# P times V with V as the loaded weights of four 32-column tiles, turned P streaming, and row sums from columns of ones

## The chip, the cores and the metric

One core of a Trainium2 chip runs the kernel; the other seven are idle. The metric is the time of one execution on the device in microseconds, the median of the runs. TensorE multiplies (one operand is loaded into the array as weights, the other streams through it), VectorE and ScalarE work on tiles in SBUF and PSUM, GpSimd on SBUF alone; the DMA queue is SyncE's.

## The reference

A cross attention and a gated feed-forward layer over 16 batches of 128 rows of width 1024, both with a residual. The attention has 32 heads of width 32 in 8 groups; the 4 heads of a group share K and V.

```python
x = x + xattn(layernorm(x), ctx, ctx, w_q, w_k, w_v, w_out, mask)
x = x + ffn(layernorm(x), w12, b12, w3, b3)

# xattn, per batch b, group g and head h of the group
scores = einsum('bghnd,bgsd->bghns', query, key) / 32 ** 0.5
scores = where(mask, scores, finfo.min)
attention = softmax(scores, axis=-1)
out = einsum('bghns,bgsd->bghnd', attention, value)
return out.transpose(0, 3, 1, 2, 4).reshape(b, n, 1024) @ w_out.T
```

The change is in `out`: softmax's division and the product with `value`.

## The kernel before

Every f32 operand is split into a high and a low f16 half, and a product is three f16 products: high by high, high by low, low by high. The kernel is written per engine, each with its own list of instructions and with semaphores between them; the order of the work is written out by hand, and is the same on all engines.

The attention runs over 8 blocks (t = 1 to 8) of U = 2 batches (256 rows), each in 8 steps s, one for each group. Group number g = 8 (t - 1) + s runs from 0 to 63. In a step TensorE does, in this order: `scores(g)` (8 matmuls, one for each batch and head, into the bank pair B_SCORE), a first product of 24 matmuls (q, o or v: a projection or the output projection of an earlier block), `turn_attn(g - 3)` at L1362, a second product, and `weigh(g - 2)` at L1412. In the last step of a block (s = 7) the two products are the two batches of the V projection, four `turn_x` calls turn the next rows, and in blocks 1 to 6 `turn_top` (L1329) and `spread_top` (L1337) turn a column of maxima into a row and spread one value over all partitions. In block 8 and three steps after it the first feed-forward products take the place of the projections. Then follow the last output projection and the feed-forward layer.

`weigh(g)` before: for each of the 2 batches and 4 heads it loads P turned (128 x 128, high and low half) as weights and streams V (32 columns, and in `v_high` a 33rd column of ones that makes the row sum), so that the result lies in B_AV with rows on partitions, 33 columns a head. It waits for the turned P (a DMA transpose), and for `s_avread`, which says that the division of the group before has read B_AV.

`divide(g)` at L1833 on VectorE: a reciprocal of the 8 row sums, then a multiplication of 256 columns into `attn` (f32, SBUF). `turn_attn(g)` transposes `attn` on TensorE into a PSUM bank, `attn_hi(g)` on ScalarE copies it as f16 into `attn_t`, `attn_lo(g)` on VectorE writes the rest that f16 lost. `out_proj(b, q)` reads `attn_t` of the 8 groups of a block as weights.

In a step VectorE does, in order: `divide(g - 3)`, `mask_scores(g)` (8 custom instructions, L1820), `gather_top` where there is one, for g up to 11 its share of `prob_lo(g - 1)` (L1830; from then on GpSimd does it all), the low half of the first product (`q_lo`, `k_lo`, `v_lo`, all L1790, or `residual`), `attn_lo(g - 3)`, extra work of some steps (`max_of`, `row_stats`, `o_low`), the low half of the second product, and `take_top`. ScalarE does the exponentials of the first batch, the high half of the first product, `attn_hi(g - 3)`, the exponentials of the second batch, the high half of the second product, and `prob_hi(g)`.

TensorE's results of all products and turns go round five PSUM banks (`banks()`, L218): a table worked out ahead gives each key in `dense_order()` (L174) the bank that has been free or held longest, and `begin` (L1319) waits until VectorE has read that bank's last content. The key ("a", g) is the turn of group g. Keys that are gone from the list change the banks of all later ones.

## Time and profile before

| | |
|---|---|
| time, median of 3 runs | 1041.52 us (1041.49 to 1042.86) |
| span of the profiled execution | 1040.4 us |
| TensorE busy | 1017.7 us (98%) |
| VectorE busy | 661.6 us (64%) |
| ScalarE busy | 447.3 us (43%) |
| GpSimd busy | 498.6 us (48%) |
| granted TensorE clock | 0.998 of full |

The time of the profiled execution is not given apart from its span, which runs from the first to the last instruction; the median of the runs is 1.1 us above it. Busy time is the time in which at least one instruction of the engine is under way. Matmuls overlap: a row with "x8" and a duration is the whole run of 8, and from one start to the next is what a matmul costs in a stream.

### The profile page before, as it was taken

How to read it: one execution, taken by the hardware profiler on the slowest of the kernel's cores; microseconds unless marked ns; L12 is line 12 of the kernel's file. 1: busy time of each engine (PE TensorE's matmuls, PEld its weight loads, DVE VectorE, ACT ScalarE, POOL GpSimd, SP SyncE). 2: the span in 40 equal slices, each digit the busy share in tenths (PEclk: the TensorE clock that was granted, in tenths of full speed). 3: DMA queues.
4: the chain of work that ended last, by engine and by line, in shares of the span. 5: the costliest groups of instructions: out<-in, count | busy, mean ns of one | idle time of the engine just before them, and what ended most of it. 6: DMA issues, size and time to landing. Idle time of an engine off the chain costs nothing.

```text
span 1040.4 us, 21876 instructions
## 1 busy us (share of the span) xinstructions
PE 1017.7 (98%) x8400; PEld 695.6 (67%) x8400; DVE 661.6 (64%) x2080; ACT 447.3 (43%) x983; POOL 498.6 (48%) x476
## 2 busy tenths in 40 slices
PE   7897999999999999999999999999999999999998
PEld 6786868869687696886655544444444888468853
DVE  6789977767787777888646234636864447625431
ACT  6768556557465574664766210123431112202100
POOL 2869923727337273379958596158742301212000
PEclk9999999999999999999999999999999999999999
DMA  9669686998989999789946715494758631974201
GB/s 367 227 160 197 168 216 168 222 247 222 248 211 229 230 245 244 179 236 232 268 94 123 253 71 203 94 345 160 272 200 185 235 112 40 236 230 122 83 31 51
DMA packets 230776, 199.12 MB, mean 191 GB/s; under 512 B 177040, under 2 KB 187280, under 8 KB 225808
## 3 DMA queue, kind: packets, MB, share of 16 engines
q1 hardware_dynamic: 230672, 197.72, 69.0%
q8 instruction: 67, 1.10, 0.4%
q14 instruction: 37, 0.30, 0.1%
HBM read 119.04 MB, written 35.65 MB: 149 GB/s over the span
## 4 chain that ended last, share of the span: by engine, by line
PE 87%; DVE 6%; DMA 1%; ACT 1%; issue 0%; SPq 0%; DVEq 0%
PE bank_dense L1349 52%; PE bank_spare L1349 13%; PE bank_score L1494 6%; PE bank_spare L1494 6%; PE bank_av L1494 3%; PE bank_score L1406 2%; DVE arena_attn L1820 2%; DVE arena_attn L1830 1%; PE bank_av L1424 1%; PE bank_av L1428 1%; PE bank_av L1426 1%; PE bank_dense L1366 1%; DMA k_scratch<-arena_in 1%; PE bank_spare L1358 0%; PE bank_dense L1358 0%
## 5 line engine op out<-in xcount | busy, mean ns | idle before, releaser
L1153 ACT ACTIVATE arena_attn<-arena_attn,arena_in 128x128 f32<-128x128 f32 x512 | 162.7, 391 | 94.6 <-DVE arena_in L1820 93.6
L1349 PE MATMUL bank_dense<-arena_rows,arena_in 128*128 128x256 f16 (+1 forms) x1272 | 175.2, 295 | 1.9 <-POOL arena_in L874 1.0
L936 POOL TENSOR_TENSOR arena_attn<-arena_attn 128x512 f16<-128x512 f32 x89 | 102.6, 1170 | 148.8 <-ACT arena_attn L1160 148.8
L1349 PE MATMUL bank_dense<-arena_attn,arena_rows 128*128 128x512 f16 x768 | 166.4, 379 | 0.0
L1349 PEld LDWEIGHTS bank_dense<-arena_rows,arena_in 128*128 128x128 f16 x1272 | 123.0, 98 | 43.1 <-DVE arena_in L1668 1.6
L1820 DVE CUSTOM_DVE_ANT_0 arena_attn<-bank_score,arena_in 128x128 f32<-128x128 f32 x512 | 143.5, 346 | 0.4 <-PE bank_score L1406 0.4
L1349 PEld LDWEIGHTS bank_dense<-arena_attn,arena_rows 128*128 128x128 f16 x768 | 75.2, 98 | 90.2
L1349 PE MATMUL bank_dense<-arena_out,arena_attn 128*128 128x512 f16 x576 | 127.8, 379 | 0.0
L1349 PEld LDWEIGHTS bank_dense<-arena_out,arena_attn 128*128 128x128 f16 x576 | 55.5, 98 | 63.3
L1349 PE MATMUL bank_spare<-arena_rows,arena_in 128*128 128x256 f16 (+1 forms) x648 | 87.6, 292 | 0.0
L1349 PE MATMUL bank_dense<-arena_out,arena_in 128*128 128x512 f16 x384 | 83.0, 379 | 0.0
L874 POOL TENSOR_TENSOR arena_in<-arena_in 128x512 f16<-128x512 f32 x62 | 74.2, 1196 | 5.0
L1349 PEld LDWEIGHTS bank_spare<-arena_rows,arena_in 128*128 128x128 f16 x648 | 63.0, 98 | 19.0
L1907 DVE SCALAR_TENSOR_TENSOR arena_out<-bank_dense,small,arena_out 128x256 f32<-128x256 f32 x64 | 28.0, 478 | 75.0 <-PE bank_dense L1349 75.0
L884 POOL TENSOR_TENSOR small<-small 128x1 f32<-128x1 f32 x32 | 19.9, 622 | 107.2 <-DVE small L1709 107.2
L1349 PEld LDWEIGHTS bank_dense<-arena_out,arena_in 128*128 128x128 f16 x384 | 37.6, 98 | 45.3
L1160 ACT ACTIVATE arena_attn<-arena_attn 128x1024 f16<-128x1024 f32 x64 | 67.2, 1050 | 1.0 <-DMA arena_attn<-arena_attn 0.7
L1349 PE MATMUL bank_dense<-arena_in 128*128 128x256 f16 x456 | 52.8, 273 | 1.4 <-DVE arena_in L1675 1.4
L1424 PE MATMUL bank_av<-v_high,arena_attn 128*128 128x33 f16 x512 | 45.5, 178 | 6.7 <-DMA arena_attn<-arena_attn 6.7
L1003 POOL TENSOR_TENSOR arena_out<-arena_out,arena_rows 128x1024 f32<-128x1024 f32 x12 | 29.2, 2462 | 47.1 <-DMA arena_out<-x_scratch 47.1
L1859 DVE SCALAR_TENSOR_TENSOR arena_rows<-bank_dense,small,arena_rows 128x256 f32<-128x256 f32 x48 | 21.0, 479 | 46.9 <-PE bank_dense L1349 43.9
L1349 PEld LDWEIGHTS bank_dense<-arena_in 128*128 128x128 f16 x456 | 43.8, 98 | 7.8 <-DVE arena_in L1675 1.7
(219 smaller groups left out, 1890.8 us busy)
## 6 DMA issues: line engine op xcount, KB each, us to landing
arena_rows<-x SPq DMA_DIRECT2D x32, 512.0 KB, 6.1
arena_in<-w_scratch SPq DMA_DIRECT2D x64, 256.0 KB, 3.1
arena_attn<-q_scratch SPq DMA_DIRECT2D x48, 256.0 KB, 4.5
arena_rows<-w_t SPq DMA_DIRECT2D x12, 1024.0 KB, 6.2
arena_rows<-ctx_t SPq DMA_DIRECT2D x8, 1024.0 KB, 6.1
q_scratch<-arena_attn SPq DMA_DIRECT2D x16, 512.0 KB, 5.1
x_scratch<-arena_rows SPq DMA_DIRECT2D x16, 512.0 KB, 3.8
arena_out<-x_scratch SPq DMA_DIRECT2D x16, 512.0 KB, 5.9
```

The source lines that it names most:

```text
L874: pool.tensor_tensor(lo, buf, hi, ALU.subtract).then_inc(ready, 1)
L936: ins = pool.tensor_tensor(p_split[:, g % 2, u, 1], e[:, g % 2, u], p_split[:, g % 2, u, 0], ALU.subtract)
L1003: ins = pool.tensor_tensor(y_res[:, u], y_res[:, u], b3_all, ALU.add)
L1153: ins = act.activation(head, head, ACT.Exp, bias=neg_max[:, g % 2, h:h + 1], scale=-1.0)
L1160: act.activation(p_split[:, g % 2, :, 0], e[:, g % 2], ACT.Copy).then_inc(s_phi, 1)
L1349: ins = pe.matmul(dst, lhs(a, c), rhs(b, c), start=(c == chunks[0] and n == 0), stop=(c == chunks[-1] and n == 2))
L1406: ins = pe.matmul(B_SCORE[:, HALF * u + SEQ * j:HALF * u + SEQ * j + SEQ], q_stack[0:3 * DH, m // 4, j, m % 4, SEQ * u:SEQ * u + SEQ], k_s ...
L1424: pe.matmul(B_AV[:, at:at + VW], prob_t[:, g % 2, u, 0, j], v_high[:, a % 2, u, m], start=True, stop=False)
L1494: ins = pe.matmul(seven(v, j), weights[:, a, P * c:P * c + P], rows[:, b, c], start=(c == 0 and n == 0), stop=(c == 3 and n == 2))
L1820: ins = dve.tensor_tensor_reduce(out=e[:, g % 2, h // HPG, SEQ * (h % HPG):SEQ * (h % HPG) + SEQ], in0=B_SCORE[:, SEQ * h:SEQ * h + SEQ], ...
L1859: ins = dve.scalar_tensor_tensor(out=cols, in0=bank("o", b, q)[:, 256 * n:256 * n + 256], scalar=c_out[:, 2 * h + n:2 * h + n + 1], in1=co ...
L1907: ins = dve.scalar_tensor_tensor(out=cols, in0=bank("y", f, q)[:, 256 * k:256 * k + 256], scalar=c_ffn[:, 2 * h + k:2 * h + k + 1], in1=co ...
```

## The change

- `weigh(g)` loads V as weights instead of P: for each batch the three products of the output (V high with P high, V high with P low, V low with P high) and two of the row sums (a block of 32 columns of ones with P high and with P low). Each is done for the 4 heads in 4 tiles of 32 columns of the array: head j writes partitions 32 j to 32 j + 31 of B_AV, 128 columns wide. The weights are 128 x 32, the streaming side is P turned, 128 x 128. That is 40 matmuls a group instead of 24. The outputs lie in columns 0 to 255 of B_AV, the sums, the same on all 32 partitions of a head, in columns 256 to 511.
- The result has heads and their columns on partitions, as `out_proj` reads it, so `turn_attn` is gone, with its entries in the orders.
- `divide(g)` takes the reciprocal of 128 x 256 sums (into `inv_rows`) and multiplies 128 x 256.
- `attn_hi(g)` and `attn_lo(g)` read `attn` in SBUF, with two semaphores of their own (`s_ahi`, `s_alo`); `out_proj` and `late_hi` wait for `s_alo`.
- `v_high` has 32 columns a group; the ones are a block of their own, set once by GpSimd.

```diff
--- before.py
+++ after.py
...
@@ -187,8 +186,6 @@
                 n.append(("h", 0, H_AT[s], 0))
-            if g >= 3:
-                n.append(("a", g - 3))
             if tile2 is not None:
@@ -198,7 +195,7 @@
     for s in (8, 9, 10):
-        n += [("h", 0, H_AT[s], 0), ("a", NG - 11 + s), ("h", 0, H_AT[s], 1)]
+        n += [("h", 0, H_AT[s], 0), ("h", 0, H_AT[s], 1)]
     n += [("o", NB - 1, q) for q in range(4)]
@@ -259,7 +256,7 @@
 SPREADS = [*FIRST_TOPS, *(key[1] for key in dense_order() if key[0] == "turn")]
-HIGHS = [key for key in dense_order() if key[0] in ("x", "a", "q", "k", "v")]
+HIGHS = [key for key in dense_order() if key[0] in ("x", "q", "k", "v")]
 
@@ -407,13 +404,15 @@
         kept, with_6, with_5, with_7 = [terms[:, 0], terms[:, 1]], terms[:, 2], terms[:, 3], terms[:, 4]
+        inv_rows = part(arena_attn, 59, 1, F32)
+        ones_wide = part(arena_attn, 60, 1)[:, 0:DH]
         k_stack = part(arena_attn, 63, 4).rearrange("p (b g n) -> p b g n", b=2, g=4)
         temp_late = part(arena_attn, 63, 2, F32)
-        v_high = sb("v_high", [P, 2, U, GROUPS, VW], F16)
+        v_high = sb("v_high", [P, 2, U, GROUPS, DH], F16)
         v_low = sb("v_low", [P, 2, U, GROUPS, DH], F16)
...
         stage.append(v_low.rearrange("p r u g w -> p (r u g w)").rearrange("p (s n) -> p s n", s=2))
-        stage.append(v_high.rearrange("p r u g w -> p (r u g w)")[:, 0:2 * HALF].rearrange("p (s n) -> p s n", s=2))
+        stage.append(v_high.rearrange("p r u g w -> p (r u g w)").rearrange("p (s n) -> p s n", s=2))
 
...
@@ -920,7 +920,7 @@
                 root(r)
-            pool.memset(v_high[:, :, :, :, DH:DH + 1], 1.0).then_inc(s_vinit, 1)
+            pool.memset(ones_wide, 1.0).then_inc(s_wide, 1)
             pool.wait_ge(*taken("q23"))
@@ -1119,10 +1119,10 @@
             def attn_hi(g):
-                act.wait_ge(s_dense, done("a", g))
+                act.wait_ge(s_avread, g + 1)
                 if g >= RING:
                     act.wait_ge(s_dense, done("o", (g - RING) // GROUPS, 3))
-                act.activation(attn_t[:, g % RING, 0], bank("a", g)[:, 0:AB], ACT.Copy).then_inc(s_dhi, 1)
+                act.activation(attn_t[:, g % RING, 0], attn, ACT.Copy).then_inc(s_ahi, 1)
 
@@ -1180,7 +1180,7 @@
                 act.wait_ge(s_w12, 28)
-                act.wait_ge(s_dense, done("a", NG - 1))
+                act.wait_ge(s_alo, NG)
                 act.activation(w12[:, 7, :, 0].rearrange("p i c o -> p i (c o)"),
...
@@ -1359,13 +1358,6 @@
 
-            def turn_attn(g):
-                pe.wait_ge(s_avread, g + 1)
-                dst = begin("a", g)
-                for u in range(U):
-                    ins = pe.transpose(dst[:, P * u:P * u + P], attn[:, P * u:P * u + P], ident[:, :])
-                ins.then_inc(s_dense, 1)
-
             def q_proj(t, m):
@@ -1418,21 +1410,22 @@
                     pe.wait_ge(*taken("ctx1"))
+                    pe.wait_ge(s_wide, 1)
                 for u in range(U):
-                    for j in range(HPG):
-                        at = VW * (HPG * u + j)
-                        pe.matmul(B_AV[:, at:at + VW], prob_t[:, g % 2, u, 0, j], v_high[:, a % 2, u, m],
-                                  start=True, stop=False)
-                        pe.matmul(B_AV[:, at:at + DH], prob_t[:, g % 2, u, 0, j], v_low[:, a % 2, u, m],
-                                  start=False, stop=False)
-                        ins = pe.matmul(B_AV[:, at:at + VW], prob_t[:, g % 2, u, 1, j], v_high[:, a % 2, u, m],
-                                        start=False, stop=True)
+                    terms_of_out = ((v_high[:, a % 2, u, m], 0), (v_high[:, a % 2, u, m], 1), (v_low[:, a % 2, u, m], 0))
+                    terms_of_sum = ((ones_wide, 0), (ones_wide, 1))
+                    for at, wanted in ((0, terms_of_out), (AB, terms_of_sum)):
+                        for n, (weights, piece) in enumerate(wanted):
+                            for j in range(HPG):
+                                ins = pe.matmul(B_AV[DH * j:DH * j + DH, at + SEQ * u:at + SEQ * u + SEQ], weights,
+                                                prob_t[:, g % 2, u, piece, j], start=n == 0, stop=n == len(wanted) - 1,
+                                                tile_position=(0, DH * j))
                 ins.then_inc(s_av, 1)
...
                 if q == 0:
-                    pe.wait_ge(s_dread, done("a", GROUPS * b + 7))
+                    pe.wait_ge(s_alo, GROUPS * b + 8)
                 if b == 0 and q == 0:
@@ -1561,8 +1554,6 @@
                         hidden(0, H_AT[s], 0)
-                    if g >= 3:
-                        turn_attn(g - 3)
                     if tile2 is not None:
@@ -1576,7 +1567,6 @@
                 hidden(0, H_AT[s], 0)
-                turn_attn(NG - 11 + s)
                 if s < 10:
@@ -1831,18 +1821,14 @@
             def divide(g):
-                av = B_AV[:, 0:VW * U * HPG].rearrange("p (h w) -> p h w", w=VW)
                 dve.wait_ge(s_av, g + 1)
-                dve.reciprocal(inv_sum[:, :].rearrange("p (h o) -> p h o", o=1), av[:, :, DH:DH + 1]).then_inc(s_inv, 1)
+                dve.reciprocal(inv_rows, B_AV[:, AB:2 * AB]).then_inc(s_inv, 1)
                 dve.wait_ge(s_inv, g + 1)
-                dve.tensor_tensor(attn.rearrange("p (h w) -> p h w", w=DH), av[:, :, 0:DH],
-                                  inv_sum[:, :].rearrange("p (h o) -> p h o", o=1).broadcast_to([P, U * HPG, DH]),
-                                  ALU.mult).then_inc(s_avread, 1)
+                dve.tensor_tensor(attn, B_AV[:, 0:AB], inv_rows, ALU.mult).then_inc(s_avread, 1)
 
             def attn_lo(g):
-                dve.wait_ge(s_dhi, hi_count("a", g))
-                dve.tensor_tensor(attn_t[:, g % RING, 1], bank("a", g)[:, 0:AB], attn_t[:, g % RING, 0], ALU.subtract)\
-                   .then_inc(s_dread, 1)
+                dve.wait_ge(s_ahi, g + 1)
+                dve.tensor_tensor(attn_t[:, g % RING, 1], attn, attn_t[:, g % RING, 0], ALU.subtract).then_inc(s_alo, 1)
```

## Rows read from the trace of the kernel before

**Rows 1.** The page's first part: busy us (share of the span) x instructions.
```profile
PE 1017.7 (98%) x8400; PEld 695.6 (67%) x8400; DVE 661.6 (64%) x2080; ACT 447.3 (43%) x983; POOL 498.6 (48%) x476
```

**Rows 2.** Busy time by stretch; columns as the first line names them.
```profile
core 0: us, PE busy (x) PEld busy (x) DVE busy (x) ACT busy (x) POOL busy (x), PEclk, DMA share, GB/s
73.00:129.00 56.00, 47.58 (x601) 41.92 (x599) 54.16 (x201) 39.52 (x99) 52.23 (x51) 1.00 0.86 188
129.00:610.00 481.00, 480.46 (x4633) 340.95 (x4634) 336.52 (x1376) 274.34 (x673) 268.94 (x282) 1.00 0.84 212
610.00:1040.00 430.00, 426.92 (x2643) 258.31 (x2640) 217.10 (x367) 84.90 (x132) 137.45 (x102) 1.00 0.52 158
```

**Rows 3.** The chain that ended last, 126 to 133 us: start, us, what.
```profile
128.24 0.13 DVE arena_in L1836
128.38 0.44 DVE arena_in L1838
...
128.87 0.44 PE bank_spare L1366 x2
129.30 2.62 PE bank_dense L1349 x24
```

**Rows 4.** Timeline of TensorE, weigh(8): start us, us, engine, line, operation, count.
```profile
131.76 0.18 PE L1424 MATMUL bank_av<-v_high,arena_attn 128*128 128x33 f16 x1
131.79 0.18 PE L1426 MATMUL bank_av<-v_low,arena_attn 128*128 128x32 f16 x1
131.81 0.18 PE L1428 MATMUL bank_av<-v_high,arena_attn 128*128 128x33 f16 x1
...
132.37 0.61 PE L1406 MATMUL bank_score<-arena_attn 96*128 96x128 f16 x8
```

**Rows 5.** Timeline of TensorE, 302.0 to 302.6 us, around one turn_attn.
```profile
302.24 0.38 PE L1366 MATMUL bank_dense<-arena_in 128*128 128x128 f32 x2
302.46 0.38 PE L1358 MATMUL bank_spare<-arena_in,arena_rows 128*128 128x128 f32 x2
```

**Rows 6.** Timeline of TensorE, 298.0 to 298.9 us, scores, turn_top, product.
```profile
298.19 0.61 PE L1406 MATMUL bank_score<-arena_attn 96*128 96x128 f16 x8
298.64 0.28 PE L1335 MATMUL bank_spare<-arena_in 128*1 128x128 f32 x1
298.75 0.38 PE L1349 MATMUL bank_spare<-arena_in 128*128 128x256 f16 x2
```

**Rows 7.** Weight loads by form: count | busy us, mean ns | idle before.
```profile
L1366 PEld LDWEIGHTS bank_dense<-arena_in 128*128 128x128 f32 x84 | 11.1, 141 | 5.0 <-DVE arena_in L1838 0.2
L1335 PEld LDWEIGHTS bank_spare<-arena_in 128*1 128x1 f32 x7 | 0.6, 84 | 0.0
```

**Rows 8.** Timeline of TensorE, 240.9 to 241.7 us, around one spread_top.
```profile
240.74 0.60 PE L1349 MATMUL bank_dense<-arena_in 128*128 128x256 f16 x4
241.27 0.38 PE L1342 MATMUL bank_dense<-small,arena_in 1*128 1x2 f32 x2
241.58 0.19 PE L1424 MATMUL bank_av<-v_high,arena_attn 128*128 128x33 f16 x1
```

**Rows 9.** VectorE by form: count | busy us, mean ns | idle before.
```profile
L1838 DVE TENSOR_TENSOR arena_in<-bank_av,arena_in 128x256 f32<-128x256 f32 x64 | 27.1, 424 | 2.2
L1836 DVE RECIPROCAL arena_in<-bank_av 128x8 f32<-128x8 f32 x64 | 12.7, 199 | 1.1
L1887 DVE RECIPROCAL small<-small 128x8 f32<-128x8 f32 x1 | 0.2, 205 | 0.0
L1895 DVE RECIPROCAL small<-small 128x1 f32<-128x1 f32 x1 | 0.2, 165 | 0.0
L1886 DVE TENSOR_SCALAR small<-small 128x8 f32<-128x8 f32 x1 | 0.2, 158 | 0.0
L1890 DVE TENSOR_SCALAR small<-small 128x1 f32<-128x1 f32 x1 | 0.2, 153 | 0.0
```

**Rows 10.** Timelines of VectorE and ScalarE in a short step, last product's halves.
```profile
320.07 0.42 DVE L1790 SCALAR_TENSOR_TENSOR arena_attn<-bank_dense,arena_attn 128x256 f16<-128x256 f32 x1 [2.06 <-ACT arena_attn L1131]
...
319.65 0.39 ACT L1131 ACTIVATE arena_attn<-bank_dense 128x256 f16<-128x256 f32 x1 [1.00 <-PE bank_dense L1349]
```

**Rows 11.** Timelines of VectorE and TensorE, last step of block 4.
```profile
302.26 0.41 DVE L1790 SCALAR_TENSOR_TENSOR v_low<-bank_spare,v_high 128x256 f16<-128x256 f32 x1
...
303.39 2.79 PE L1349 MATMUL bank_dense<-arena_in 128*128 128x256 f16 x24
```

More of the change, by code:

```diff
@@ L49 @@
 EPS = 1e-5
-VW = DH + 1
 EXPONENT = 0x7F800000
@@ L534, in xattn_ffn @@
         s_pool = sem("pool_chain")
-        s_ident, s_ones, s_vinit, s_mask_add = sem("ident_done"), sem("ones_done"), sem("v_init_done"), sem("mask_done")
+        s_ident, s_ones, s_wide, s_mask_add = sem("ident_done"), sem("ones_done"), sem("wide_ones_done"), sem("mask_done")
         s_rload = [sem("even_rows_loaded"), sem("odd_rows_loaded")]
@@ L559, in xattn_ffn @@
         s_av, s_inv, s_avread = sem("av_done"), sem("inv_sum_done"), sem("attn_ready")
+        s_ahi, s_alo = sem("attn_hi_done"), sem("attn_lo_done")
         s_scales, s_cout = sem("block_scales_done"), sem("c_out_done")
@@ L1228, in _ @@
             o_sum(3)
-            act.wait_ge(s_vinit, 1)
             v_hi(0, 0)
```

## The prediction, made before the changed kernel was run

> **What bounds the kernel now.** I read the page's first part, then busy time by stretch, then the chain that ended last. TensorE is busy 1017.7 of 1040.4 us [rows 1], but a share over the whole span says little about one stage. By stretch [rows 2] there are three regimes. From 73 to 129 us VectorE is busy 54.16 of 56.00 us and TensorE 47.58: the first attention steps are VectorE's. From 129 to 610 us TensorE is busy 480.46 of 481.00 and VectorE 336.52: a microsecond of TensorE work is a microsecond of time there, and VectorE has air. From 610 us on nothing that the diff touches runs. The chain says the same and names the hand-over [rows 3]: VectorE's pieces follow each other until the division of group 7 at 128.38, for which turn_attn(7) waits at 128.87; from there it is TensorE to the end. So there are two accounts: VectorE work in the first 8 divisions (groups 0 to 7), TensorE work in the 56 calls of weigh after the hand-over (groups 8 to 63) and the 57 turns (groups 7 to 63).
>
> **What goes from TensorE.** weigh(8) starts at 131.76 and the scores after it at 132.37 [rows 4]: 24 matmuls with their 24 weight loads in 0.61 to 0.62 us, a start every 25.5 to 25.8 ns, although one matmul lasts 177 ns: they are pipelined. A turn of one group starts at 302.24 and the next work at 302.46 [rows 5]: 0.22 us. So 56 x 0.62 = 34.7 us and 57 x 0.22 = 12.5 us go, 47.2 us.
>
> **What comes on TensorE.** 40 matmuls a group: per batch 3 x 4 for the output and 2 x 4 for the sums, 32 columns of weights, 128 columns streaming. No row of before shows two column tiles next to each other, so the pace is bounded from both sides.
> - Upper end, one tile after another: the 8 score matmuls also stream 128 columns, from 298.19 to 298.64 [rows 6]: 56 ns each, so 40 x 0.056 = 2.24 us a group.
> - Lower end, the four tiles side by side with nothing else in the way: 10 quartets x 56 ns = 0.56 us. The loads hardly limit it: a load of 1 column lasts 84 ns, of 128 f32 columns 141 ns [rows 7], so 57/127 = 0.45 ns a column and 14 ns for 32 columns, 0.57 us for 40 loads.
> - Between them is the pace that the trace has for a load with a matmul, whatever it streams: 25.8 ns is the shortest spacing, at 32 and 33 streamed columns, which alone would be 33/128 of 56 = 14 ns. That looks like a cost of issue that tiles share. 40 x 25.8 = 1.03 us a group. I take this one: it is the nearest row in kind (small f16 matmuls, each with its own load), and the stream of 56 ns is covered by the three issues for the other tiles.
>
> At 1.03 us, 56 groups cost 57.8 us: TensorE's account is 57.8 - 47.2 = +10.6 us.
>
> **Switching the tiles.** Each weigh now enters and leaves another tiling of the array. The trace has two analogues. turn_top loads one column of weights, for which the program sets a 32-column tile: scores 298.19, turn_top 298.64, the next product 298.75 [rows 6]; 0.45 us for the scores and 0.11 for the turn are the plain paces, so nothing is lost. spread_top has one row, a 32-row tile: it starts at 241.27, the last product matmul before it (the fourth of a piece begun at 240.74, at 0.109 us each) at 241.07, weigh follows at 241.58 [rows 8], and before each there is idle time that no semaphore explains: against 0.11 and two issues of 0.026 some 0.35 us is lost. The column case is the nearer one (same kind of tile, in and out), so I take 0; 0.35 is the other bound. The page "TensorEngine Tiling (Array Packing)" of the Trainium skill (Key Properties) says that changing the tiling mode drains TensorE; spread_top agrees with it, turn_top doesn't show it. By that page each weigh would pay, which is the second rival.
>
> **What VectorE gains in work.** The reciprocal grows from 8 to 256 elements a partition. Two rows on small data give the slope [rows 9]: 165 ns at 128x1, 205 ns at 128x8, 5.7 ns an element, while a plain tensor_scalar takes 153 and 158 ns for the same sizes, 0.7 ns an element. So a wide reciprocal costs 165 + 255 x 5.7 = 1.62 us against 0.20 now (x64): +1.42 us a group. Bounds: 0.43 us at 1.04 ns an element (the 256 elements of the multiplication in 424 ns, less its fixed part of about 157), and, as the slope comes from 7 elements and one run each, 2.3 us at half as much again. The multiplication keeps its size. attn_lo and attn_hi read SBUF instead of PSUM at the same 256 columns; both take about 0.4 us now and I change neither.
> In the stretch before the hand-over VectorE sets the end, and all 8 divisions there lie on the chain: 8 x 1.42 = 11.4 us. The ninth follows a step that is full too (a weight split, row statistics): 0.6 more, 12 us together. TensorE's 0.2 us a group there lies in its 8 us of idle time, and costs nothing.
> After the hand-over the steps have room: in a typical one VectorE waits 2.06 us for ScalarE, which itself waits 1.00 us for TensorE [rows 10]. The longer division is hidden there. What is queued behind it on VectorE: the masked scores, for which ScalarE's exponentials and the next scores wait, and the low halves that free PSUM banks. The place without room is the last step of a block (s = 7). There VectorE goes through division, masking, the gathered maximum and v_lo without a gap, v_lo from 302.26 to 302.67, and TensorE starts the second V product at 303.39 [rows 11]. Without the turns the planner gives this product the bank of the first V product, so it waits for v_lo at 302.67 + 1.42 = 304.1, while TensorE would be there at 303.2: 0.9 us, in the 5 blocks t = 2 to 6 that gather a maximum, less what TensorE's own delay gives back: 4 us. At 0.43 us for the reciprocal this is 0, at 2.3 it is 8.
>
> **What else moves.** The wait of turn_attn for the division goes (0.61 us at the hand-over, in rows 3's chain); late next is the mask behind it on VectorE, so nothing is won. attn_hi waits for the division instead of the turn, and out_proj for attn_lo directly; they were ready a product earlier, off the chain. The ones are now a memset of 32 columns instead of a strided column. No DMA changes.
>
> **Sum.** 1040.4 (span) + 10.6 + 12 + 4 = 1067.0, and 1.1 for what lies between the span and the median of the runs (1041.52): 1068.
>
> **Rivals.**
> 1. One tile after another: the column tiles take turns. For it: no row shows two tiles at work together. Weigh takes 2.24 us, 56 x 2.24 - 47.2 = +78; the first stretch +12 to +14, no stall at s = 7 since TensorE is later itself: 1132.
> 2. The switch of tiles costs what spread_top pays, 0.35 us x 56 = +20, less the stalls at s = 7 that it covers (-1): 1087.
> 3. Side by side beyond the issue pace, ending on the other side: 0.56 us a weigh, 56 x 0.56 - 47.2 = -15.9 on TensorE. "TensorE: Matmul & The Clock Gate" of the Trainium skill (Part 3, packing small matmuls) has tiles start about 4 ns apart and three column tiles give 2.38 times the speed; no row here shows it. With VectorE's +12 and stalls of 5 to 6 (TensorE gives none back) this is 1043. It turns faster than before once the reciprocal takes under about 1.5 us instead of 1.62: then VectorE's terms are below 15.9. At 0.43 us the time would be 1028.
> 4. The reciprocal streams at one element a cycle, with the pace of issue: +10.6 + 2: 1054. Against it stands the slope in rows 9.
>
> **Chances.** Forecast 0.43, within 1058 to 1078. Rival 1: 0.21. Rival 2: 0.13. Rival 3: 0.16, of which half is faster, a quarter the same. Rival 4: 0.07. Faster by over 0.2% 0.09 (half of rival 3, and 0.01 for rivals 3 and 4 between them meeting half-way), within 0.2% 0.04, slower 0.87; 0.2% is about what a measurement can tell from no change. The range leaves out half of rival 1 (0.1) and the lower two thirds of rival 3 (0.1): 1043 to 1132.
>
> **What would show it.** In the trace after: the time from the first matmul of weigh to the next scores, 1.03 us (0.56, 1.4 and 2.24 in the rivals), with no idle time before or behind; the reciprocal of 128x256 at 1.6 us; the hand-over from VectorE to TensorE some 12 us later than 129 us, one group on at most; TensorE waiting for v_lo once a block at s = 7 by under 1 us; the last 430 us unchanged. Wrong would be: a TensorE clock that falls in the attention blocks (it is 1.00 in all stretches of rows 2), or VectorE bound in every block, which would need a reciprocal of 3 us or more.

## The result, and the profile of the changed kernel

The changed kernel takes 1071.32 us (median of 4 runs, 1069.84 to 1080.96); the kernel before, run beside it, 1042.19. The ratio is 1.0288, with a 95% interval of 1.026 to 1.0316: slower by 29 us by the medians and 30 by the ratio. The forecast was 1068, within 1058 to 1078. Its total is nearly right, and its account is not: TensorE's term was about 14 us too high and the waits after the hand-over about 17 us too low, and it is luck that the two cancel. The runs below show this.

The page's first part and the shares of its chain, beside [rows 1]:

```profile
PE 1024.1 (96%) x9296; PEld 678.8 (63%) x9296; DVE 761.0 (71%) x2080; ACT 443.2 (41%) x983; POOL 497.8 (47%) x476
...
PE 57%; DVE 25%; ACT 6%; DMA 4%; issue 3%; SPq 1%; POOL 1%; DVEq 0%; ACTq 0%
```

TensorE has 896 matmuls more and is busy only 6.4 us more in a span of 1070.4 us, so it waits longer than before. VectorE has 99.4 us more, and a quarter of the chain that ended last is now its own, where it was 6%.

Busy time by stretch, with the columns of [rows 2]. The first stretch is the one of [rows 2], the last one is shifted by 30 us, and the second begins at 207 us; the kernel before has for it the line that stands first:

```profile
207.00:610.00 403.00, 402.46 (x3817) 281.37 (x3816) 277.55 (x1123) 227.80 (x553) 236.27 (x245) 1.00 0.84 215
```
```profile
73.00:129.00 56.00, 42.64 (x579) 35.03 (x580) 53.14 (x168) 33.03 (x80) 45.75 (x47) 0.91 0.71 160
...
207.00:610.00 403.00, 389.17 (x4432) 263.07 (x4431) 357.52 (x1165) 228.00 (x568) 227.88 (x237) 0.99 0.84 206
...
640.00:1070.00 430.00, 426.95 (x2643) 258.35 (x2641) 215.15 (x367) 84.87 (x132) 136.29 (x101) 1.00 0.52 158
```

The last 430 us are as before. In the attention blocks TensorE, which before idled 0.5 of 403 us, now idles 14, and in the first stretch its granted clock falls to 0.91.

One weigh on TensorE, against [rows 4]: start, us, line, operation, count.

```profile
217.74 2.78 PE L1348 MATMUL bank_dense<-arena_in 128*128 128x256 f16 x24
220.45 0.29 PE L1420 MATMUL bank_av<-arena_attn,v_high 128*32 128x128 f16 x8
220.57 0.23 PE L1420 MATMUL bank_av<-arena_attn,v_low 128*32 128x128 f16 x4
220.63 0.28 PE L1420 MATMUL bank_av<-arena_attn 128*32 128x128 f16 x8
...
221.14 0.61 PE L1398 MATMUL bank_score<-arena_attn 96*128 96x128 f16 x8
```

From the first matmul of weigh to the scores it takes 0.69 us for 40 matmuls. The row of the ones starts 3 quartets after that of v_high, at 0.18 us; the whole is 10 quartets of 56 ns, 0.56 us, with 0.13 us behind them. The four tiles of a quartet start 3 to 4 ns apart, so they stream side by side. The product ahead of weigh would be through at 217.74 + 24 x 0.109 = 220.36, and weigh starts at 220.45: another 0.09 us. So a group costs TensorE 0.56 + 0.22 = 0.78 us, where it was 0.62 + 0.22 = 0.84 us before [rows 4, 5].

VectorE by form, against [rows 9] (the multiplication takes 424 ns as before):

```profile
L1825 DVE RECIPROCAL arena_attn<-bank_av 128x256 f32<-128x256 f32 x64 | 111.9, 1748 | 1.0
L1831 DVE TENSOR_TENSOR arena_attn<-arena_in,arena_attn 128x256 f16<-128x256 f32 x64 | 33.0, 515 | 19.5 <-ACT arena_attn L1125 19.5
```

The reciprocal takes 1748 ns instead of 199, 64 times: 99 us, all of VectorE's increase.

What TensorE waited for from 142 to 540 us: releaser, then us in total, times, longest. The kernel before has one such wait for VectorE in that stretch, of 0.4 us:

```profile
PE bank_spare L1358 <- DVE v_low L1790: 0.4, 1, 0.4
```

The changed kernel:

```profile
PE bank_dense L1357 <- DVE small L1608: 4.8, 3, 2.0
PE bank_dense L1348 <- DVE v_low L1780: 3.4, 4, 2.2
PE bank_spare L1348 <- DVE arena_attn L1831: 2.0, 3, 1.2
PE bank_score L1398 <- DVE arena_in L1810: 1.9, 2, 1.3
PE bank_spare L1357 <- DVE small L1608: 1.0, 1, 1.0
PE bank_av L1420 <- DVE arena_in L1827: 0.9, 1, 0.9
PE bank_spare L1348 <- DVE v_low L1780: 0.8, 2, 0.4
```

With three smaller rows (0.7, 0.6 and 0.5 us) this is 16.6 us. L1357 is turn_x, and L1608 the gathered maximum (`gather_top`), which has to read the PSUM bank that turn_x writes next; L1831 is attn_lo, for which out_proj waits; L1810 is the mask and L1827 the division. The wait for v_lo, the one that the prediction names, is 4.2 us of it. By place, 10.1 us lie in the last step of the blocks (s = 7) and the rest in the steps s = 2 to 4, most of it in blocks 2 and 7.

The delay against the kernel before, read at the start of the scores of the first group of each block (t = 1 to 8), is 1.9, 11.4, 14.8, 16.4, 18.9, 21.5, 23.2 and 30.3 us, and 30.0 at the last scores. In steps without a stall the changed kernel is 0.04 to 0.05 us a step quicker.

### The profile page after: what moved, and what is told of

Same layout as the page of the kernel before. It is cut to its first block, busy times and chain, and to the rows that moved or that the text cites. A ratio compares the mean times of both kernels' runs of the same rounds, so it can differ in the third digit from the quotient of the medians.

```text
span 1070.4 us, 23604 instructions
## 1 busy us (share of the span) xinstructions
PE 1024.1 (96%) x9296; PEld 678.8 (63%) x9296; DVE 761.0 (71%) x2080; ACT 443.2 (41%) x983; POOL 497.8 (47%) x476
## 4 chain that ended last, share of the span: by engine, by line
PE 57%; DVE 25%; ACT 6%; DMA 4%; issue 3%; SPq 1%; POOL 1%; DVEq 0%; ACTq 0%
PE bank_dense L1348 35%; DVE arena_attn L1825 6%; DVE arena_attn L1810 6%; PE bank_spare L1348 6%; PE bank_score L1487 6%; PE bank_spare L1487 5%; ACT arena_attn L1153 3%; DMA arena_rows<-w_t 3%; PE bank_av L1487 3%; DVE arena_in L1646 2%; DVE arena_attn L1820 2%; DVE small L1690 1%; DVE arena_attn L1831 1%; DVE arena_attn L1780 1%; PE bank_av L1420 1%
## 5 line engine op out<-in xcount | busy, mean ns | idle before, releaser
L1153 ACT ACTIVATE arena_attn<-arena_attn,arena_in 128x128 f32<-128x128 f32 x512 | 162.6, 389 | 214.6 <-DVE arena_in L1810 214.6
L1348 PE MATMUL bank_dense<-arena_rows,arena_in 128*128 128x256 f16 (+1 forms) x1200 | 164.7, 296 | 1.9 <-POOL arena_in L874 1.0
L1810 DVE CUSTOM_DVE_ANT_0 arena_attn<-bank_score,arena_in 128x128 f32<-128x128 f32 x512 | 143.4, 344 | 1.2 <-PE bank_score L1398 1.2
L1825 DVE RECIPROCAL arena_attn<-bank_av 128x256 f32<-128x256 f32 x64 | 111.9, 1748 | 1.0
L1348 PE MATMUL bank_dense<-arena_out,arena_attn 128*128 128x512 f16 x456 | 101.1, 379 | 1.3 <-DVE arena_out L1672 0.7
L1348 PE MATMUL bank_spare<-arena_rows,arena_in 128*128 128x256 f16 (+1 forms) x720 | 97.9, 294 | 0.0
L1348 PEld LDWEIGHTS bank_spare<-arena_rows,arena_in 128*128 128x128 f16 x720 | 69.9, 98 | 24.1
L1348 PEld LDWEIGHTS bank_dense<-arena_out,arena_attn 128*128 128x128 f16 x456 | 43.8, 98 | 52.3 <-DVE arena_attn L1831 1.1
L1348 PE MATMUL bank_dense<-arena_in 128*128 128x256 f16 x576 | 70.2, 281 | 6.4 <-DVE v_low L1780 4.9
L1348 PE MATMUL bank_spare<-arena_out,arena_attn 128*128 128x512 f16 x312 | 70.8, 384 | 2.0 <-DVE arena_attn L1831 2.0
L1348 PEld LDWEIGHTS bank_dense<-arena_in 128*128 128x128 f16 x576 | 57.3, 101 | 17.8 <-DVE v_low L1780 6.1
L1348 PEld LDWEIGHTS bank_spare<-arena_out,arena_attn 128*128 128x128 f16 x312 | 30.2, 99 | 37.3 <-DVE arena_attn L1831 2.6
```

Of the source, the lines that this page charges most:

```text
L1153: ins = act.activation(head, head, ACT.Exp, bias=neg_max[:, g % 2, h:h + 1], scale=-1.0)
L1348: ins = pe.matmul(dst, lhs(a, c), rhs(b, c), start=(c == chunks[0] and n == 0), stop=(c == chunks[-1] and n == 2))
L1810: ins = dve.tensor_tensor_reduce(out=e[:, g % 2, h // HPG, SEQ * (h % HPG):SEQ * (h % HPG) + SEQ], in0=B_SCORE[:, SEQ * h:SEQ * h + SEQ], ...
L1825: dve.reciprocal(inv_rows, B_AV[:, AB:2 * AB]).then_inc(s_inv, 1)
```

## The experiments

Theory A: TensorE loses nothing by the change, and the whole 29 us are VectorE's wide reciprocal, through the first stretch and through waits later. Its rival B is the prediction's account, where about a third of the time is TensorE's own. The first kernels take the reciprocal out of the changed kernel, and put it alone into the kernel before.

### The changed kernel with a narrow reciprocal

It reads 8 columns instead of 256; the rest of the inverse is set to one, so that most of the division is left out.

```diff
...
-                dve.reciprocal(inv_rows, B_AV[:, AB:2 * AB]).then_inc(s_inv, 1)
+                dve.reciprocal(inv_rows[:, 0:8], B_AV[:, AB:AB + 8]).then_inc(s_inv, 1)
```

> The changed kernel, but the reciprocal takes 8 of the 256 columns; the other reciprocals are ones set once, so the division by the row sums is left out for them. The multiplication keeps its size, TensorE does the same work. Theory A (all of the loss is VectorE's longer reciprocal; on TensorE the new weigh is a little cheaper than the old weigh with its turn, -0.05 us a group as unstalled steps show): 64 x -0.05 = -3 us against the kernel before, 1037 to 1041 us. Theory B (the split of the forecast, TensorE +0.19 us a group): +10.6 us, 1050 to 1054. Theory C (the loss lies in the lower clock or the DMA queue, not in the reciprocal): 1060 or more.

Measured: 1041.92 us (10 runs) against 1042.55 (13 runs), ratio 0.9987 (0.997 to 1.0004). The time is that of the kernel before, with the 40 matmuls and the switches of tiles all in place. Its reciprocal, and what is left of TensorE's waits for VectorE from 142 to 540 us (3.2 us):

```profile
L1828 DVE RECIPROCAL arena_attn<-bank_av 128x8 f32<-128x8 f32 x64 | 12.8, 200 | 1.1
```
```profile
PE bank_spare L1358 <- DVE small L1609: 1.7, 1, 1.7
PE bank_dense L1349 <- DVE v_low L1781: 1.1, 1, 1.1
PE bank_spare L1349 <- DVE v_low L1781: 0.4, 1, 0.4
```

So everything but the reciprocal is worth nothing that can be measured, and account B falls: without VectorE's terms it gives 1052. Theory A had 1037 to 1041, a gain of 3 us on TensorE; the ratio puts the difference at -1.4 us (-3.1 to +0.4), and the waits that are left take up such a gain in this execution.

### The kernel before with a wide reciprocal besides

A reciprocal of 256 columns, whose result nobody reads, runs ahead of the narrow one.

```diff
...
+                dve.reciprocal(wide, B_AV[:, 0:AB]).then_inc(s_inv, 1)
                 dve.reciprocal(inv_sum[:, :].rearrange("p (h o) -> p h o", o=1), av[:, :, DH:DH + 1]).then_inc(s_inv, 1)
...
```

> The kernel before, with one reciprocal of 128x256 more in each division, into a place that nobody reads: VectorE's new cost alone, 1.55 to 1.75 us a group, TensorE unchanged, the turns still there. Theory A: 30 to 40 us slower than the kernel before, 1072 to 1082, with TensorE waiting at the turn as well. Theory B (forecast: 12 us in the first stretch, 4 at the ends of blocks): 1056 to 1061.

Measured: 1076.55 us, ratio 1.0313 (1.0275 to 1.0351). Its rows of the reciprocals and, over the whole run, its two largest waits of TensorE for VectorE:

```profile
L1837 DVE RECIPROCAL arena_attn<-bank_av 128x256 f32<-128x256 f32 x64 | 112.0, 1750 | 1.0
L1838 DVE RECIPROCAL arena_in<-bank_av 128x8 f32<-128x8 f32 x64 | 9.3, 145 | 0.0
```
```profile
PE bank_dense L1367 <- DVE arena_in L1840: 9.4, 7, 3.8
PE bank_spare L1367 <- DVE arena_in L1840: 5.9, 8, 2.7
```

VectorE's cost alone, in a kernel whose TensorE work is that of before, makes the whole loss and somewhat more, as theory A has it. The reciprocals take 1.90 us a group here, 1.70 more than before, and 1.55 more in the changed kernel. The largest waits sit at L1367, turn_attn, which the changed kernel no longer has; from 142 to 540 us TensorE waits 16.2 us for VectorE in all, where the changed kernel has 16.6.

### The tiles one after another in the program

Head by head instead of product by product over the four heads: the three products of a head's output, then the next head's, and after them the two products of each head's sums in the same way.

```diff
-                        for n, (weights, piece) in enumerate(wanted):
-                            for j in range(HPG):
+                        for j in range(HPG):
+                            for n, (weights, piece) in enumerate(wanted):
```

> The changed kernel with the same 40 matmuls in another order: all products of one column tile follow each other (3 for the output, 2 for the sums), then the next tile's. Theory D (tiles work side by side only if neighbours in the order are of different tiles; a tile starts its next matmul 55 ns after its last): 24 neighbours of the same tile a group, weigh takes 24 x 55 ns = 1.3 us instead of 0.56, and the time grows by 56 x 0.75 = 42 us less what TensorE's present waits for VectorE (about 20 us) cover: 1090 to 1110. Theory E (the order does not matter, TensorE takes any free tile): weigh stays at 0.56 to 0.7 us, 1071. Theory F (a tile is loaded slowly after its own matmul, with no overlap): 2.2 us and more, 1130 or more.

Measured: 1075.32 us (one run; the changed kernel's runs reach from 1069.84 to 1080.96), which rules out theories D and F. Weigh on TensorE:

```profile
219.74 0.32 PE L1420 MATMUL bank_av<-arena_attn,v_high 128*32 128x128 f16 x8
219.86 0.25 PE L1420 MATMUL bank_av<-arena_attn,v_low 128*32 128x128 f16 x4
219.91 0.30 PE L1420 MATMUL bank_av<-arena_attn 128*32 128x128 f16 x8
...
220.43 0.62 PE L1398 MATMUL bank_score<-arena_attn 96*128 96x128 f16 x8
```

It is again 0.69 us to the scores, and the records come in the order of the quartets, although the program lists them head by head. Within a quartet the starts are now 10 ns apart instead of 3 to 4, which fits an issue of three instructions for one tile before the next tile's, and the steps without a stall are 0.02 us longer than in the changed kernel. So at this depth the order in the program costs next to nothing: the records look as if each tile went on by itself. This takes rival 1 out (tiles in turn, 2.24 us a weigh), for either order.

### A second switch inside weigh

One full 128 x 128 matmul between the two batches, so that each weigh leaves its tiling and enters it again.

```diff
                 for u in range(U):
+                    if u:
+                        pe.matmul(B_AV[:, SEQ:2 * SEQ], prob_t[:, g % 2, 1, 0, 0], prob_t[:, g % 2, 1, 0, 1],
+                                  start=True, stop=True)
```

> The changed kernel with one 128x128 matmul over the full array between the two batches of a weigh (its result is overwritten): one more change out of the 32-column tiles and back. Theory G (a change between full array and column tiles costs 0.23 us a pair, as the time around weigh suggests): from the first matmul of weigh to the scores 0.69 + 0.055 + 0.23 = 0.97 us, time 1078 to 1088. Theory H (the losses at the ends are something else, changing tiles is free as turn_top showed): 0.75 us, time 1071 to 1075.

Measured: 1080.97 us (one run, which alone tells little, since one of the changed kernel's took 1080.96). The batches' seam in weigh, and the scores behind it:

```profile
220.82 0.28 PE L1423 MATMUL bank_av<-arena_attn 128*32 128x128 f16 x8
221.03 0.23 PE L1416 MATMUL bank_av<-arena_attn 128*128 128x128 f16 x1
221.19 0.30 PE L1423 MATMUL bank_av<-arena_attn,v_high 128*32 128x128 f16 x8
...
221.59 0.62 PE L1398 MATMUL bank_score<-arena_attn 96*128 96x128 f16 x8
```

Weigh began at 220.64, so it takes 0.95 us instead of 0.69. Of the 0.26 us more, 0.056 is the matmul itself; 0.21 is the pair of switches, the same as the 0.22 read in the changed kernel. The prediction's value of 0 for it, from turn_top, is wrong, and its bound of 0.35, from spread_top, is 0.13 too high. The rule of the Trainium skill, page "TensorEngine Tiling (Array Packing)", Key Properties, that a change of the tiling mode drains TensorE, is borne out for these column tiles; turn_top, which loads one column [rows 6], does not show it, and why is open.

### Where in the run the wide reciprocal costs

Two kernels share the 64 groups between them: the wide reciprocal in groups 0 to 7 alone, and in groups 8 to 63 alone. In the first one the later groups keep the columns 8 to 255 of group 7's inverse, not ones as its expectation says; the instructions and their sizes are the same either way.

The edit against the kernel with the narrow reciprocal, and then the second against the first:

```diff
...
-                dve.reciprocal(inv_rows[:, 0:8], B_AV[:, AB:AB + 8]).then_inc(s_inv, 1)
+                n = AB if g < 8 else 8
+                dve.reciprocal(inv_rows[:, 0:n], B_AV[:, AB:AB + n]).then_inc(s_inv, 1)
```

> As the narrow reciprocal, but the first 8 groups have the full 256 columns; from group 8 on 8 columns and ones, so that division is left out there. It prices the first stretch alone, which the forecast put at 8 x 1.42 = 11.4 us; with the measured 1.75 us the same step gives 8 x 1.55 = 12.4 us. Theory A: 1042 + 11 to 13 = 1053 to 1055 us. Theory L (the block-by-block starts are right that only 9.5 us come in block 1 and 3.4 in block 2, and a late VectorE catches up in block 2): 1050 to 1052.

Measured: 1052.66 us, ratio 1.0089 (1.0058 to 1.0121): +9.3 us. That lies between theory L's 8 to 10 and theory A's 11 to 13 and rules out neither. Its block 2 starts 9.2 us behind the kernel before, block 4 starts 11.6 us behind, and the last scores 9.5.

```diff
...
-                n = AB if g < 8 else 8
+                n = AB if g >= 8 else 8
...
```

> The complement of the kernel with the wide reciprocal in the first 8 groups: here groups 0 to 7 take the reciprocal of 8 columns (the other columns of the inverse are ones, so the division is left out there), and groups 8 to 63 take all 256. Theory M (the two costs add: what the first 8 wide reciprocals cost, 9.3 us, and what the other 56 cost are separate): after less 9.3, about 1062, +20 against before; the start of the scores of block 2 some 1.5 us behind before instead of 11.4, and the stalls in the last steps of the blocks as in the changed kernel. Theory N (the late start of the changed kernel caused part of the stalls further on, since each engine reaches block 2 already behind): 1052 to 1056, with fewer or shorter stalls in blocks 2 to 7.

Measured: 1063.15 us against 1043.87, ratio 1.0198 (1.0154 to 1.0243): +20.7 us by the ratio. 9.3 and 20.7 are 30, the whole of it: the two costs add (theory M), within the 5 us or so that the two intervals leave, and theory N's 1052 to 1056 is outside (1060 to 1069 by the interval). So the late start of block 2 doesn't make the later stalls. The profiled execution took 1071.95 us, the longest of the four, so the places of its stalls aren't typical in size; its block 2 starts 3.6 us behind. Of VectorE's terms the forecast had 12 and 4.

### Half the width

128 columns in all 64 groups; the other half of the division is left out.

```diff
...
-                dve.reciprocal(inv_rows, B_AV[:, AB:2 * AB]).then_inc(s_inv, 1)
+                dve.reciprocal(inv_rows[:, 0:SEQ], B_AV[:, AB:AB + SEQ]).then_inc(s_inv, 1)
```

> The changed kernel with the reciprocal of 128 of the 256 columns in all 64 groups (the other half of the inverse is ones, so that half of the division is left out). Duration: if each element costs the same, 199 + (1748 - 199) x 120/248 = 0.95 us. Theory P (the cost in time is proportional to the reciprocal's length, since the chain in the steps alternates through VectorE anyway): half of the 29 us that the wide one costs, 1056 to 1058. Theory Q (a slack in the steps: only what exceeds it counts; the first 8 groups have none and cost half of 9.3 us, the later ones are covered): 1046 to 1049, TensorE's stalls in the last steps of the blocks nearly gone.

Measured: 1055.42 us, ratio 1.0127 (1.0094 to 1.016), +13 us: the total of theory P, and Q's is outside the interval.

```profile
L1828 DVE RECIPROCAL arena_attn<-bank_av 128x128 f32<-128x128 f32 x64 | 60.8, 949 | 1.0
```
```profile
PE bank_dense L1349 <- DVE v_low L1781: 1.6, 3, 1.0
PE bank_score L1399 <- DVE arena_in L1811: 1.3, 1, 1.3
PE bank_spare L1349 <- DVE v_low L1781: 0.8, 2, 0.4
PE bank_spare L1358 <- DVE small L1609: 0.8, 1, 0.8
PE bank_spare L1349 <- DVE arena_attn L1834: 0.7, 1, 0.7
```

Where the time sits speaks partly for Q, though. These waits, again from 142 to 540 us, are 5.2 us where the full width has 16.6 and 8 columns have 3.2, so in the later blocks the first 0.75 us of a longer reciprocal cost 2 us and the next 0.80 us cost 11.4. In this execution, the shortest of the four (1053.03 us), block 2 starts 8.2 us late and the last scores are 11.0 us late. What neither theory has is that half the width costs 7.5 us in block 1, where the full width costs 9.5; with 8 columns that block came out at 1.7 (first kernel) and 4.2 us (wide from group 8 on) in one execution each, so it varies by more than 2 us, and I can't divide it further.

### Two ways to take the load off VectorE

The low half of the divided result (attn_lo) of groups 8 to 51 on GpSimd, placed behind the prob_lo of its step in GpSimd's order; the division of the next group waits for it:

```diff
+            def attn_lo(g):
+                if g not in ALO_AWAY:
+                    return
+                pool.wait_ge(s_ahi, g + 1)
+                pool.wait_ge(s_alo, g)
+                pool.tensor_tensor(attn_t[:, g % RING, 1], attn, attn_t[:, g % RING, 0], ALU.subtract).then_inc(s_alo, 1)
...
```

> The changed kernel with attn_lo of groups 8 to 51 on GpSimd (both operands lie in SBUF now): 0.5 us less on VectorE in 44 groups, a division more that waits for GpSimd. Theory A (after the first stretch the loss is VectorE's backlog at the ends of blocks, 15 to 18 us of the 30): a third of the added 1.55 us is given back there, 1062 to 1067 us. Theory J (the steps are tied through ScalarE's waits for the masked scores, not through VectorE's sum of work, or GpSimd is late): 1069 to 1073.

Measured: 1089.88 us, ratio 1.0444 (1.0406 to 1.0482), slower than the changed kernel; both expectations missed. TensorE's longest waits are new ones:

```profile
PE bank_dense L1358 <- POOL arena_attn L946: 10.8, 3, 3.8
...
PE bank_spare L1358 <- POOL arena_attn L946: 5.0, 2, 3.8
```

L946 is attn_lo on GpSimd, 717 ns each. Four of these waits, 3.4 to 3.8 us, are at s = 3 of blocks 3 to 6, where out_proj needs attn_lo. GpSimd had no idle time before it there: it works without a break through the split of the next context (L872 to L876) and prob_lo (L938), and attn_lo stands behind them. In block 4 TensorE starts at 286.36, as soon as this has ended:

```profile
285.63 0.67 POOL L946 TENSOR_TENSOR arena_attn<-arena_in,arena_attn 128x256 f16<-128x256 f32 x1
```

I had counted its length and not its place. Another place in that order wasn't tried.

The inverse on ScalarE as exp(-ln(sum)), with the reciprocal gone; VectorE divides behind the masking instead of ahead of it:

```diff
...
+                act.activation(inv_rows, B_AV[:, AB:2 * AB], ACT.Ln).then_inc(s_inv, 1)
+                act.wait_ge(s_inv, 2 * g + 1)
+                act.activation(inv_rows, inv_rows, ACT.Exp, scale=-1.0).then_inc(s_inv, 1)
...
```

> The changed kernel with the inverse of the row sums on ScalarE, as exp(-ln(sum)) in two instructions of 128x256 (0.27 to 0.4 us each), and the division after the masking on VectorE. VectorE then has less to do than in the kernel before (no reciprocal at all, -0.2 us), ScalarE 0.6 us a group more at 41% busy. Theory A: TensorE bound from about 125 us on, with its -0.05 us a group: 1036 to 1041 us, at or a little under the kernel before. Theory K (ScalarE takes over as the late engine, since the exponentials of a step follow the inverse): 1045 to 1060. If the two functions lie in different tables, a reload of 1.28 us for each would show as 1100 and more.

Measured: 1083.44 us, ratio 1.038 (1.0344 to 1.0417), above theories A and K and below the 1100 that the reloads were put at. The two table loads of each group, and the wait for the inverse that results:

```profile
L1125 ACT ACT_TABLE_LOAD x64 | 82.1, 1283 | 1.1
L1127 ACT ACT_TABLE_LOAD x64 | 82.1, 1283 | 1.1
```
```profile
DVE arena_in L1837 <- ACT arena_attn L1127: 81.2, 42, 4.3
```

The two functions themselves take 384 and 417 ns; each brings a table load of 1283 ns along, so the inverse takes 3.4 us of ScalarE, against 1.75 on VectorE. The Trainium skill, page "ScalarE: Activation LUTs", section on table sets, has a set that holds exp and ln together and counts one load for ln followed by exp; here each of the two is preceded by a load of its own.

No version that ran beats the kernel before. The best case, with a reciprocal of 200 ns, equals it.

## Why the prediction was right in its total and wrong in its terms

1. **What bounds the kernel** (VectorE until 129 us, TensorE after it, the last 430 us untouched): right as a reading of the kernel before. After the change the second part no longer holds; "VectorE bound in every block would need a reciprocal of 3 us or more" is where it went wrong (point 5).

2. **TensorE's account, forecast +10.6 us.** The step that failed is the choice of 25.8 ns a matmul, "a cost of issue that tiles share". The quartets go by at 56 ns, 14 ns a matmul: rival 3's pace, the lower bound. The four starts of a quartet are 3 to 4 ns apart, so 25.8 ns is no cost of issue. That pace [rows 4] was one of 128-column weight loads, each with a short stream; whether the loads set it, no run shows. A group costs 0.78 us where 0.84 us went: -0.06 us, and 56 x -0.06 = -3.4 us. The steps without a stall show -0.04 to -0.05. The term was too high by 14 us.

3. **Switching, forecast 0.** It is 0.09 us in and 0.13 out, 0.22 a weigh; 56 x 0.22 = 12.3 us, so rival 2's mechanism is real, at two thirds of its price. Of the two analogues the one of the same kind of tile misled: it is one matmul with one column, and no run shows why it pays nothing.

4. **VectorE in the first stretch, forecast +12.** The mechanism was right: 9.3 us measured alone, 9.5 in block 1 of the changed kernel. The slope that gave 1.62 us for the reciprocal was nearly right: 1748 ns, 6.2 ns an element between 8, 128 and 256 elements instead of 5.7. The eight divisions are 12.4 us more work, so about 3 us of them were covered. Block 1 varies by some 2 us from one execution to another, so these 3 us are rough.

5. **Waits after the hand-over, forecast 4 us.** The wait that was named is there, and that its sum is 4.2 us is chance: it is 0.40 us in each of the five blocks named, where 0.9 was expected, and 2.2 us in block 7, which was not named. The step that failed is "the longer division is hidden there". It leant on VectorE's wait of 2.06 us for ScalarE [rows 10], but a step is a loop: VectorE divides and masks, ScalarE takes the exponentials and the halves, VectorE the low halves. Its room is the last wait in it for something outside, which is ScalarE's 1.00 us for TensorE in the same rows. 1.55 us more don't fit into 1.00. In a stretch of short steps the chain that ended last no longer goes through TensorE at all:

```profile
259.18 1.77 DVE arena_attn L1825
...
262.82 0.97 ACT arena_attn L1153 x3
...
266.25 1.68 DVE arena_attn L1825
...
269.80 0.97 ACT arena_attn L1153 x3
...
273.24 1.67 DVE arena_attn L1825
```

   From reciprocal to reciprocal it is 6.98 us, where TensorE's step is 6.47. At half the width the same reciprocals start 6.19 and then 6.37 us apart, less than TensorE's step, so nothing builds up. An estimate from the 6.98 and 6.47: the loop would just keep pace with a reciprocal 0.51 us shorter than 1.75, which is 1.04 us more than the 0.20 of before. This agrees with the room of 1.00.

   In blocks 3 to 6 the reciprocal starts 0.55, 1.07 and 1.59 us after the scores of its step in the first three steps, and 4.9 in the fourth; at half the width these are 0.56, 0.28, 0.19 and 3.2, before 0.53, 0.35, 0.34 and 2.1 (1.9 in one block). So the lag builds up step by step. TensorE pays where something is due that stands behind the division on VectorE: turn_x for the bank of the gathered maximum (5.8 us), out_proj for attn_lo (2.6), the scores for the mask (1.9), besides v_lo. At turn_x the lag is handed on in full. Block 4:

```profile
314.52 0.62 PE L1398 MATMUL bank_score<-arena_attn 96*128 96x128 f16 x8
316.58 1.75 DVE L1825 RECIPROCAL arena_attn<-bank_av 128x256 f32<-128x256 f32 x1
321.20 0.66 PE L1357 MATMUL bank_dense<-arena_in,arena_rows 128*128 128x128 f32 x4 [2.01 <-DVE small L1608]
```

   In the last step of blocks 2 to 6 the reciprocal starts 0.19, 1.05, 2.05, 1.96 and 0.86 us after the scores, and turn_x waits 0.15, 1.00, 2.01, 1.92 and 0.82: 0.04 to 0.05 less each time. The wide reciprocal alone uses up this step's room, and every lag that arrives there is added. The one such wait at half the width, 0.77 us, fits as well: 1.62 us late, less 0.04, less the 0.80 by which its reciprocal is shorter.

   ScalarE's exponentials wait for the mask 214.6 us in all, 93.6 before. I had looked for the place without room, the last step of a block, and priced one wait there as if VectorE arrived in time; the lag reaches it from the steps before, and reaches other waits too. The waits at half the width, 5.2 us instead of 16.6, agree. How the 4.9 us of the fourth step become the 0.9 to 2.1 us of the last is not followed here.

6. **The clock.** I expected 1.00 in all stretches. After an idle time of TensorE, products run in part at the lower of its two levels (1.2 GHz instead of 2.4):

```profile
530.32 4.25 PE L1348 MATMUL bank_dense<-arena_in 128*128 128x256 f16 x24 [2.16 <-DVE v_low L1780]
```

   These 24 matmuls take 2.78 us at the full level, so the stall of 2.16 us cost another 1.5. The mean granted clock of the changed kernel is 0.989 in the profiled execution, 0.998 with the narrow reciprocal. In the stretch from 207 to 610 us a clock of 0.99 is at most 4 us of the 18.6 that come after block 1. In the first stretch 0.91 is at most 5 us, in part while TensorE has little to do, and how much of the 9.5 us in block 1 it makes no run separates. So the measured cost of a stall holds some of this, and where a sum counts the waits alone it is short.

The sum as read in the changed kernel's profiled execution: about -3 on TensorE, +9.5 for the first block and +21 later, which is the 18.6 us after block 1 with TensorE's 3 put back; TensorE's waits for VectorE make 16.6 of it, from 142 to 540 us, and the lower clock up to 4 us. The forecast was +10.6, +12 and +4. Errors of 14 and 17 us cancelled, and that is why the total came out. Rival 3 had the right pace at a chance of 0.16, and its time of 1043 was wrong twice: it left out the switch of tiles (12 us) and took the later waits at 5 to 6 us.

## What to carry to other kernels

Price the elementwise work that a layout brings along before the matmuls that it saves: sums that come out the same on 32 partitions made 8 reciprocals a row into 256, and this alone cost 3%. When you look whether a longer instruction is hidden, go round the whole loop of engines that it is part of, and take as its room the wait of the last engine in it for something outside the loop, not the wait of the engine that gets longer; once the room is used up, follow the lag to the steps that have none left, where it is added to TensorE's waits in full, and expect the clock to take its share. Column tiles of one weigh run side by side whatever their order in the program, for a price of about 0.2 us for entering and leaving them.

## What the runs showed of the hardware

- Four 32-column tiles stream together: a quartet of 128-column matmuls every 56 ns, starts 3 to 4 ns apart, weight loads of 32 columns hidden. With the program's order turned round it is 56 ns again, with starts 10 ns apart.
- Going from full-width matmuls to column tiles and back costs 0.21 to 0.22 us.
- A reciprocal on VectorE takes 200 ns for 8 elements a partition, 949 for 128 and 1748 for 256: 6.2 ns an element, where a multiplication of 256 takes 424 in all.
- attn_lo, now with both operands in SBUF, has a median of 415 ns, as before from PSUM (414, never above 425), but a mean of 515 and up to 1277, where GpSimd runs beside it. From the timelines of VectorE and GpSimd in the changed kernel:

```profile
466.52 0.98 DVE L1831 TENSOR_TENSOR arena_attn<-arena_in,arena_attn 128x256 f16<-128x256 f32 x1
...
466.18 1.04 POOL L870 TENSOR_TENSOR arena_in<-arena_rows,small 128x512 f32<-128x512 f32 x1
```

  VectorE's instruction ends 0.28 us after the first one on GpSimd. So do all 19 of the 64 that take over 430 ns (0.278 to 0.284 us after an instruction of GpSimd), whenever they started: most of the work is done only when the other has ended. In the kernel before, with one operand in PSUM, 35 of the 64 ran beside GpSimd's instructions and none was slowed. The Trainium skill, page "SBUF — State Buffer", section "SBUF: two separate sides", agrees: the two engines share a pair of ports, locked for a whole instruction, which VectorE takes when it reads two inputs from SBUF. It costs 6.4 us of VectorE's time here (64 x 0.1), and more in the kernel with the narrow reciprocal, which is none the slower for it.
